# Latent attention with a factored feed-forward layer on one core: the order of work at a unit's boundary, and pair 0's weights later in the start-up

## The chip, the cores and the metric

The kernel runs on one core of one Trainium2 chip. The metric is the device time of one launch in microseconds (us). Engines are called as in the profile: PE is TensorE, PEld its weight loads, DVE is VectorE, ACT is ScalarE, POOL is GpSimd, SP is SyncE, which issues nearly all DMAs here.

## The reference, cut to what matters

```python
xn = layernorm(x)                               # x: 1 x 2048 x 512
q = (xn @ wq)            -> 16 heads, 128 (nope) + 64 (rope)
kva = xn @ wkv_a         -> ckv (128), k_pe (64)
ckv = ckv * rsqrt(mean(ckv^2) + 1e-6) * kv_norm_scale
kv = (ckv @ wkv_b)       -> 16 heads, k_nope 128 + v 128
q_pe, k_pe = rope(q_pe), rope(k_pe)
scores = (q_nope k_nope^T + q_pe k_pe^T) / sqrt(192), causal
out = softmax(scores) @ v                       # 16 heads x 128
attn = out @ wo
mixed = sum over 8 factors of xn @ factors[r], / sqrt(8) + bias
return x + attn + mixed
```

## The kernel before

The weights are absorbed. For a head h, w_abs = wq_nope[h] x wkv_b_k[h] takes the normalized x straight to a query of the 128-wide latent, and w_vo = wkv_b_v[h] x wo[h] takes the latent output straight to the 512-wide result, so all heads share one set of keys (kTh, kTl, the rope part kRh, kRl) and values (vH, vL). Every operand is split into a high and a low half-precision part, and a product is three matmuls (`three`, L358 to L360: high x high, high x low, low x high); the products w_abs, w_vo and the output projection use the fp32r format.

*Start-up.* A loop of steps t = 0 to 19 on every engine. A step normalizes and transposes one tile of 128 rows of x, and two steps later projects it to the latent (L429); every second step finishes a pair of tiles: scaling, rope, keys (L439), values. Between these, in fixed steps, stands the preparation of head pair 0: GpSimd's `scale_keys(0)` (L1179), ScalarE's `squares` of the weights (L646), TensorE's `norm` sum over partitions (L395), VectorE's `row_powers` and `scale_pair` (L841 to L867), the transposes of wq and wkv_b (L377, L384), `w_abs` and `w_pe`. GpSimd meanwhile adds up the eight factors of the feed-forward layer (L1160).

*Units.* A unit i is one head of one chunk of 512 queries: 64 units, chunks in the order 3, 2, 1, 0, sixteen heads each. A unit has four rows r of 128 queries. Chunk 3 sees 2048 keys, four pieces of up to 512 a row; chunk 0 sees up to 512, one piece a row. For each piece TensorE makes scores (L493 to L499) in one of four score banks, VectorE takes the maximum (L1017, the masked last piece L1019), after the last piece the row maximum (L1029) and the exponential's bias nm (L1035), ScalarE the exponential (`exps`, L703) and its half-precision high part (`high_parts`, L713), GpSimd the low part (`low_parts`, L1218), and SP issues the DMA that transposes both into pT. The values product of unit i-1 (tiles pT, vH, vL) runs in the later rows of unit i and ends in its row 3 with one bank of outputs. `read_output` then splits it: ScalarE casts the high part into oT (L720), VectorE subtracts for the low part (L1048). In rows 0 to 3 of unit i+1 TensorE makes the four output projections of that head (`head_output`, tiles wV, oT), and VectorE accumulates each into the result (L1062).

*The order of the work.* Each engine runs its own instruction list in order, and only semaphores tie the lists together. What is not scores, maxima, exponentials or low parts comes from one function, `fills(i, r)`: the list of extra work of row r of unit i, behind the row's main work. Every engine walks the same list and takes the kinds that concern it: "q" (the next unit's query: TensorE projects it, tiles xT, wA; ScalarE casts, L686; VectorE forms the low part, L994), "pe" (rope queries of a pair), "parts" (their parts: ScalarE L692, GpSimd L1209), "out" (an output projection), "pv" (the values product and, at its end, `read_output`), "den" (denominators), and, in the first sixteen units only, the preparation of later heads' weights: "wo" (ScalarE's cast of wo, L682) and "wo_low" (GpSimd's low part of it, L1190), "wvo" (TensorE's w_vo product, tiles wV, wKV; VectorE's split of it, L937), "tq", "tkv", "wabs", squares ("sqk", "sq0", "sq1", "sqp"), "nrm", "wpe". The three PSUM banks for this work rotate in the order of the same list (`bank_order`): each use waits for VectorE to have read the use three before. In unit 0 stands the feed-forward product, whose weights follow from the squares of the summed factors ("sqf", "nf").

ScalarE differs in one point: in rows 0 and 1 of a unit with three or four pieces, it does the row's extra work after its third exponential (p == 2), in front of the fourth (L798 to L800). VectorE does all extra work after the row's maxima and nm (L1141 to L1145), so the low part of an output stands at the end of row 3, in front of the next unit's row 0 (L1070 to L1072).

Of the kernel before, what the change touches and what calls it, by code (L numbers as in the profile page):

```python
# [35 lines left out]
NU = NC * H  # L36
# [50 lines left out]
def fills(i, r):  # L87

    out = []
    if r == 0:  # L90
        if 1 <= i <= H:
            out.append(("wo", i - 1))
# [4 lines left out]
    if r == 0:  # L97
        if i + 1 < NU:
            out.append(("q", i + 1))
        if i + 2 <= H + 2:  # L100
            out.append(("tkv", i + 2))
        if i % 2 == 0 and i + 2 < H:
            out += [("sqk", i + 2), ("r8", i + 2)]
        if i == 0:
            out.append(("sqf", 0))
        if i // H == NC - 1 and i + 1 < NU and (i + 1) % H:
            out.append(("parts", i + 1))
# [5 lines left out]
    if r == 1:  # L113
        if i % 2 == 0 and i + 2 < H:
            out += [("nrm", i + 2), ("wpe", i + 2)]
        if i == 0:
            out.append(("nf", 0))
        if i + 2 < H:
            out.append(("tq", i + 2))
        if 1 <= i <= NU:  # L120
            out.append(("den", i - 1))
        if i // H < NC - 1 and i + 1 < NU and (i + 1) % H:
            out.append(("parts", i + 1))
        if 1 <= i <= H:
            out.append(("wo_low", i - 1))
        if i % 2 and i + 3 < H:
            out.append(("sqp", i + 3))
# [32 lines left out]
def bank_order():  # L160

    pre = []
    for t in range(NT + 4):
        if t < NT:
            pre.append(("xt", t))
        if t == 0:
            pre.append(("na", 0))
        if t == 3:
            pre.append(("nrm", 0))
        if t in (4, 8):  # L170
            pre += [("tq", t // 4 - 1), ("tkv", t // 4 - 1)]
        if t in (6, 10):
            pre.append(("wabs", t // 4 - 1))
        if t % 2 == 1 and 0 <= t // 2 - 2 < NP:
            pre.append(("kT", t // 2 - 2))
        if t == NT + 1:
            pre.append(("pe", 0))
        if t == NT + 2:
            pre.append(("q", 0))
# [4 lines left out]
def build(nc, x, wq, wkv_a, wkv_b, wo, kvs, factors, bias, rope_t, rope_n, out):  # L184
    ctx = ExitStack()
    with ctx:
# [169 lines left out]
        def _(e):  # L356
# [201 lines left out]
            for t in range(NT + 4):  # L558
# [5 lines left out]
                if t == 3:  # L564
                    norm(("nrm", 0), ("a_sqp", "a_sq0", "a_sq1", "v_r8"), nrm[:, :])
                if t in (4, 8):
                    wq_transpose(t // 4 - 1)
                    kv_transpose(t // 4 - 1)
                if t in (6, 10):
                    w_abs(t // 4 - 1)  # L570
# [18 lines left out]
        def _(e):  # L589
# [164 lines left out]
            for t in range(NT + 4):  # L754
# [12 lines left out]
                if t == 2:  # L767
# [4 lines left out]
                if t == 3:  # L772
                    squares("sq1", 0)
                    squares("sqp", 0)
                if t == 8:
                    w_pe(0)
# [14 lines left out]
            for i in range(NU + 2):  # L791
                for r in range(QT):
                    last = chunk(i) if i < NU else -1
                    for p in range(last + 1):
# [3 lines left out]
                        if p == 2 and r < 2:  # L798
                            for kind, n in fills(i, r):
                                fill(kind, n)  # L800
                    if last >= 0:
                        high_parts(i, r, last)
                    if last < 2 or r >= 2:
                        for kind, n in fills(i, r):
# [4 lines left out]
        def _(e):  # L809
# [255 lines left out]
            def fill(kind, n):  # L1065
# [4 lines left out]
                elif kind == "pv":  # L1070
                    if n[1].stop == QT * (chunk(n[0]) + 1):
                        read_output(n[0])  # L1072
# [27 lines left out]
            for t in range(NT + 4):  # L1100
# [11 lines left out]
                if t == 2:  # L1112
# [3 lines left out]
                if t == 3:  # L1116
                    scale_pair(0)
                if t in (4, 8):
                    wq_transpose(t // 4 - 1)
                    kv_transpose(t // 4 - 1)  # L1120
                if t in (6, 10):
                    w_abs(t // 4 - 1)
                if t % 2 == 0 and 0 <= p - 2 < NP:
                    value_parts(p - 2)
                if t == 9:
# [12 lines left out]
            for i in range(NU + 2):  # L1138
                for r in range(QT):
# [4 lines left out]
                    for kind, n in fills(i, r):  # L1144
# [4 lines left out]
        def _(e):  # L1149
# [63 lines left out]
            def low_parts(i, r, p):  # L1213
# [18 lines left out]
                            pattern=[[-1, CH]], channel_multiplier=1).then_inc(z["g_const"], 1)  # L1232
            for i in range(NF):
                factor(i)
                if i == KE + 3:
                    scale_keys(0)
# [278 lines left out]
```

## Time and profile before

| | us |
|---|---|
| median of 3 runs | 1705.14 (1702.17 to 1706.04) |
| profiled execution | 1705.76 |
| its span | 1703.7 |
| TensorE, VectorE, ScalarE, GpSimd busy | 1547.7, 1012.0, 955.6, 913.3 |
| mean granted TensorE clock | 0.979 |

The span is the time from the first to the last instruction of the profiled execution. "Idle before" in a row is the time in which the engine stood still before the instruction, with what ended it; "issue" means that the profile shows no releaser. Times of a row in a timeline are its start and its duration.

### The profile page before, as it was taken

The numbers are of one execution on the slowest core, as the hardware profiler recorded it, in microseconds if no ns is written. First come the engines' busy times: TensorE is split into PE (matmuls) and PEld (weight loads), VectorE is DVE, ScalarE is ACT, GpSimd is POOL, SyncE is SP. The second block draws the span as 40 slices with busy tenths as digits, with TensorE's granted clock in tenths as the row PEclk, the third lists the DMA queues.
The fourth block names the chain that finished last, engine by engine and source line by source line (L and its number), as shares of the span: only waits on it lengthen the run. The fifth ranks groups of instructions, "written<-read, shape, count | busy, mean of one in ns | idle before, by whom it ended". The sixth has DMA issues, their size and how long they took to land.

```text
span 1703.7 us, 25255 instructions
## 1 busy us (share of the span) xinstructions
PE 1547.7 (91%) x7876; PEld 821.2 (48%) x7876; DVE 1012.0 (59%) x2356; ACT 955.6 (56%) x2329; POOL 913.3 (54%) x897
## 2 busy tenths in 40 slices
PE   4779899999999999999999999999999999988887
PEld 3534454544445454444444454444444544444444
DVE  5855566565665665556555565556556665656666
ACT  5654656666666556655665656655455555443443
POOL 3555555655556555565555565556445555443443
PEclk9889999999999999999999999999999999999999
DMA  8626676777677778677786777967656668454554
GB/s 276 210 43 137 127 152 145 155 146 152 146 143 142 144 155 185 136 157 152 159 158 140 143 144 132 192 131 174 128 132 133 135 133 168 112 134 94 112 113 119
DMA packets 646883, 246.68 MB, mean 145 GB/s; under 512 B 599392, under 2 KB 612192, under 8 KB 646112
## 3 DMA queue, kind: packets, MB, share of 16 engines
q1 hardware_dynamic: 646752, 245.08, 67.5%
q8 instruction: 65, 1.06, 0.3%
q14 instruction: 66, 0.54, 0.1%
HBM read 79.30 MB, written 23.07 MB: 60 GB/s over the span
## 4 chain that ended last, share of the span: by engine, by line
PE 74%; DVE 9%; issue 8%; ACT 7%; POOL 1%; DMA 1%; SPq 0%; ACTq 0%; DVEq 0%; POOLq 0%
PE ps L358 16%; PE ps L360 15%; PE ps L359 15%; PE ps L493 6%; PE ps L498 6%; PE ps L499 6%; PE ps L494 6%; PE ps L495 6%; ACT ex L703 4%; DVE gm L1017 2%; DVE ps L1019 2%; DVE acc L1062 1%; ACT q L686 1%; DVE nm L1035 1%; ACT st L713 0%
## 5 line engine op out<-in xcount | busy, mean ns | idle before, releaser
L1218 POOL TENSOR_TENSOR st<-ex,st 128x512 f16<-128x512 f32 (+3 forms) x640 | 636.8, 1013 | 635.9 <-ACT st L713 625.4
L703 ACT ACTIVATE ex<-ps,nm,scales 128x512 f32<-128x512 f32 (+3 forms) x640 | 452.0, 708 | 610.3 <-DVE nm L1035 610.3
L713 ACT ACTIVATE st<-ex 128x512 f16<-128x512 f32 (+3 forms) x640 | 342.1, 561 | 6.1 <-ACT ex L703 0.4
L1017 DVE TENSOR_REDUCE gm<-ps 128x1 f32<-128x512 f32 (+1 forms) x384 | 248.6, 667 | 141.5 <-PE ps L499 139.8
L493 PE MATMUL ps<-kTh,q 128*128 128x512 f16 (+3 forms) x640 | 225.4, 352 | 16.3 <-ACT ex L703 12.4
L498 PE MATMUL ps<-kRh,q 128*128 128x512 f16 (+3 forms) x640 | 223.9, 350 | 3.7 <-POOL q L1209 3.7
L494 PE MATMUL ps<-kTl,q 128*128 128x512 f16 (+3 forms) x640 | 224.4, 351 | 0.0
L495 PE MATMUL ps<-kTh,q 128*128 128x512 f16 (+3 forms) x640 | 224.1, 350 | 0.0
L499 PE MATMUL ps<-kRl,q 128*128 128x512 f16 (+3 forms) x640 | 223.9, 350 | 0.0
L358 PE MATMUL ps<-pT,vH 128*128 128x512 f16 (+3 forms) x640 | 223.2, 349 | 0.0
L359 PE MATMUL ps<-pT,vH 128*128 128x512 f16 (+3 forms) x640 | 222.2, 347 | 0.0
L360 PE MATMUL ps<-pT,vL 128*128 128x512 f16 (+3 forms) x640 | 218.9, 347 | 0.0
L358 PE MATMUL ps<-wV,oT 128*128 128x512 f32 x256 | 131.8, 515 | 72.9 <-issue 67.6
L1062 DVE SCALAR_TENSOR_TENSOR acc<-ps,rden,acc 128x512 f32<-128x512 f32 x256 | 189.5, 742 | 14.0 <-PE ps L360 13.6
L1209 POOL TENSOR_TENSOR q<-rot,q 32x512 f16<-32x512 f32 x128 | 149.2, 1166 | 63.4 <-ACT q L692 51.5
L994 DVE SCALAR_TENSOR_TENSOR q<-ps,q 128x512 f16<-128x512 f32 x64 | 44.2, 691 | 194.9 <-ACT q L686 194.9
L1019 DVE CUSTOM_DVE_ANT_0 ps<-ps,cmask 128x256 f32<-128x256 f32 (+3 forms) x256 | 132.3, 517 | 28.4 <-PE ps L499 25.3
L1048 DVE TENSOR_TENSOR oT<-ps,oT 128x512 fp32r<-128x512 f32 x64 | 44.2, 691 | 137.2 <-ACT oT L720 137.2
L703 ACT ACTIVATION_READ_ACCUMULATOR ex<-ps,nm,scales 128x1 f32 x640 | 125.2, 196 | 0.0
L493 PEld LDWEIGHTS ps<-kTh,q 128*128 128x128 f16 x640 | 62.9, 98 | 95.2 <-ACT ex L703 24.4
L358 PE MATMUL ps<-xT,wA 128*128 128x512 f16 x256 | 104.7, 409 | 0.0
L360 PE MATMUL ps<-wV,oT 128*128 128x512 f32 x256 | 102.7, 401 | 0.0
(187 smaller groups left out, 2307.5 us busy)
## 6 DMA issues: line engine op xcount, KB each, us to landing
wV<-w_vo SPq DMA_DIRECT2D x48, 512.0 KB, 3.6
wA<-w_abs SPq DMA_DIRECT2D x48, 256.0 KB, 2.9
pT<-st SPq DMA_TRANSPOSE x640, 3.2
early<-factors_in SPq DMA_DIRECT2D x32, 256.0 KB, 3.7
w_vo<-wV SPq DMA_DIRECT2D x16, 512.0 KB, 3.1
wP<-w_pe SPq DMA_DIRECT2D x24, 256.0 KB, 3.0
wsq<-wq_in SPq DMA_DIRECT2D x16, 256.0 KB, 3.5
wso<-wo_in SPq DMA_DIRECT2D x16, 256.0 KB, 2.8
```

Of the source, the lines that this page charges most:

```text
L358: e.matmul(o, a[0], b[0], start=first, stop=False)
L359: e.matmul(o, a[0], b[1], start=False, stop=False)
L360: return e.matmul(o, a[1], b[0], start=False, stop=last)
L493: e.matmul(b, q[:, i % 2, 0, qs], kTh[:, ks], start=True, stop=False)
L494: e.matmul(b, q[:, i % 2, 0, qs], kTl[:, ks], start=False, stop=False)
L495: e.matmul(b, q[:, i % 2, 1, qs], kTh[:, ks], start=False, stop=False)
L498: e.matmul(b, q[:, i % 2, 2, qs], kRh[:, ks], start=False, stop=False)
L499: e.matmul(b, q[:, i % 2, 2, qs], kRl[:, ks], start=False, stop=True).then_inc(z["p_s"], 1)
L703: e.activation(ex[:, n % NEX, 0:keys], s_bank(n)[:, 0:keys], ACT.Exp, bias=nm[:, (i * QT + r) % 4:(i * QT + r) % 4 + 1], scale=scales[:, p ...
L713: e.activation(stage(n, keys)[:, :, 0, :], ex[:, n % NEX, 0:keys].rearrange("p (t n) -> p t n", n=P), ACT.Copy).then_inc(z["a_pH"], 1)
L1017: e.tensor_reduce(m, b, AX_X, ALU.max).then_inc(z["v_max"], 1)
L1218: e.tensor_tensor(s[:, :, 1, :], ex[:, n % NEX, 0:keys].rearrange("p (t n) -> p t n", n=P), s[:, :, 0, :], ALU.subtract).then_inc(z["g_pL" ...
```

## The change

- `fills`: in row 0 "q" now stands before "wo" and "out", on every engine that follows the list and in the rotation of the PSUM banks. "wo_low" goes from row 1 to row 0.
- VectorE: the output's low part leaves the end of row 3 and follows the next unit's row 0 maxima and nm. In units 0 to 15 it then takes "out" before the other kinds; in units 16 and later it follows the list, "q" before "out".
- ScalarE: in front of the fourth exponential of rows 0 and 1 it keeps only "q", "wo" and "parts"; other kinds follow the row.
- GpSimd: `scale_keys(0)` stands before the first factor sum instead of among them.
- Start-up: pair 0's squares go from steps 2 and 3 to 3 and 5, the norm and the pair's scales from 3 to 7, the row powers from 2 to 4, the transposes of wq and wkv_b from 4 and 8 to 5 and 9, w_abs from 6 and 10 to 8 and 11, w_pe from 8 (ScalarE) and 9 (VectorE) to 12 and 13.

```diff
@@ fills(i, r)
     if r == 0:
+        if i + 1 < NU:
+            out.append(("q", i + 1))
         if 1 <= i <= H:
-            out.append(("wo", i - 1))
+            out += [("wo", i - 1), ("wo_low", i - 1)]
     if i == NU - 1:
         out += [("out", (i - 2) * QT + t) for t in range(QT) if r == 3]
     elif 2 <= i:
         out.append(("out", (i - 2) * QT + r))
     if r == 0:
-        if i + 1 < NU:
-            out.append(("q", i + 1))
...
-        if 1 <= i <= H:
-            out.append(("wo_low", i - 1))
@@ start-up, TensorE (bank_order, ScalarE and VectorE alike)
-                if t == 3:
-                    norm(("nrm", 0), ("a_sqp", "a_sq0", "a_sq1", "v_r8"), nrm[:, :])
-                if t in (4, 8):
+                if t in (5, 9):
                     wq_transpose(t // 4 - 1)
                     kv_transpose(t // 4 - 1)
-                if t in (6, 10):
-                    w_abs(t // 4 - 1)
+                if t == 7:
+                    norm(("nrm", 0), ("a_sqp", "a_sq0", "a_sq1", "v_r8"), nrm[:, :])
+                if t in (8, 11):
+                    w_abs(t // 3 - 2)
@@ ScalarE, units
                         if p == 2 and r < 2:
+
                             for kind, n in fills(i, r):
-                                fill(kind, n)
+                                if kind in ("q", "wo", "parts"):
+                                    fill(kind, n)
                     if last >= 0:
                         high_parts(i, r, last)
-                    if last < 2 or r >= 2:
-                        for kind, n in fills(i, r):
+                    for kind, n in fills(i, r):
+                        if last < 2 or r >= 2 or kind not in ("q", "wo", "parts"):
                             fill(kind, n)
@@ VectorE, fill and units
-                elif kind == "pv":
-                    if n[1].stop == QT * (chunk(n[0]) + 1):
-                        read_output(n[0])
...
                         row_max(i, r)
-                    for kind, n in fills(i, r):
+                    if r == 0 and 2 <= i:
+                        read_output(i - 2)
+
+                    for kind, n in sorted(fills(i, r), key=lambda work: i < H and work[0] != "out"):
                         fill(kind, n)
@@ GpSimd
+            scale_keys(0)
             for i in range(NF):
                 factor(i)
-                if i == KE + 3:
-                    scale_keys(0)
```

## Rows read from the trace of the kernel before

**Rows 1.** The page's busy times: us (share of the span) xinstructions.
```profile
PE 1547.7 (91%) x7876; PEld 821.2 (48%) x7876; DVE 1012.0 (59%) x2356; ACT 955.6 (56%) x2329; POOL 913.3 (54%) x897
```
**Rows 2.** Waits of TensorE, 160:721, 721:1686, 1686:1704: us in total, times, longest.
```profile
PE ps L358 <- issue: 28.7, 23, 2.1
PE ps L493 <- ACT ex L703: 8.6, 14, 0.8
...
PE ps L358 <- issue: 60.7, 33, 3.3
PE ps L498 <- POOL q L1209: 1.6, 1, 1.6
...
PE ps L358 <- DVE oT L1048: 2.9, 2, 1.5
```
**Rows 3.** TensorE's groups, 160:721, then 721:1686: busy, mean ns | idle before.
```profile
L358 PE MATMUL ps<-wV,wKV 128*128 128x512 f32 x15 | 7.2, 480 | 20.7 <-issue 20.7
...
L358 PE MATMUL ps<-wV,oT 128*128 128x512 f32 x189 | 98.1, 519 | 60.4 <-issue 59.7
```
**Rows 4.** Timeline of a unit boundary, 817 to 823: start us, us.
```profile
817.49 0.27 PE L499 MATMUL ps<-kRl,q 128*128 128x256 f16 x1
...
818.09 0.59 ACT L720 ACTIVATE oT<-ps 128x512 fp32r<-128x512 f32 x1
818.72 0.69 DVE L1048 TENSOR_TENSOR oT<-ps,oT 128x512 fp32r<-128x512 f32 x1 [3.83 <-ACT oT L720]
...
819.51 0.47 PE L358 MATMUL ps<-wV,oT 128*128 128x512 f32 x1 [1.75 <-issue]
...
820.28 0.39 PE L358 MATMUL ps<-xT,wA 128*128 128x512 f16 x1
...
820.39 0.42 DVE L1019 CUSTOM_DVE_ANT_0 ps<-ps,cmask 128x256 f32<-128x256 f32 x1
...
821.09 0.22 DVE L1035 SCALAR_TENSOR_TENSOR nm<-rm,scales,head 128x1 f32<-128x1 f32 x1
...
822.88 0.38 PE L493 MATMUL ps<-kTh,q 128*128 128x512 f16 x1
```
**Rows 5.** Timeline at a w_vo product.
```profile
436.73 1.26 POOL L1190 TENSOR_TENSOR wV<-wso,wV 128x512 fp32r<-128x512 f32 x1
...
438.09 0.47 PE L358 MATMUL ps<-wV,wKV 128*128 128x512 f32 x1 [1.71 <-issue]
```
**Rows 6.** 13 stretches with a low clock: busy by engine, granted clock, DMA; one and their sum.
```profile
1585.20:1588.60 3.40, 1.42 (x4) 0.80 (x5) 1.17 (x4) 1.97 (x5) 1.16 (x1) 0.83 0.78 186
...
sum 44.30, PE 25.86 PEld 15.13 DVE 26.39 ACT 19.94 POOL 26.44; mean PE 1.99 PEld 1.16 DVE 2.03 ACT 1.53 POOL 2.03
```
**Rows 7.** Timeline of a unit boundary of the last chunk.
```profile
1584.53 0.22 PE L499 MATMUL ps<-kRl,q 128*128 128x128 f16 x1
...
1586.39 0.69 DVE L1048 TENSOR_TENSOR oT<-ps,oT 128x512 fp32r<-128x512 f32 x1 [1.48 <-ACT oT L720]
...
1587.18 0.56 PE L358 MATMUL ps<-wV,oT 128*128 128x512 f32 x1 [2.44 <-issue]
```
**Rows 8.** VectorE's group of the query's low part, 721:1700.
```profile
L994 DVE SCALAR_TENSOR_TENSOR q<-ps,q 128x512 f16<-128x512 f32 x46 | 31.8, 691 | 131.0 <-ACT q L686 131.0
```
**Rows 9.** Timeline, row 1's last scores of an even unit.
```profile
422.16 0.28 PE L493 MATMUL ps<-kTh,q 128*128 128x256 f16 x1 [0.76 <-ACT ex L703]
```
**Rows 10.** Waits of TensorE, 0:160.
```profile
PE ps L493 <- ACT ex L703: 3.8, 4, 2.0
```
**Rows 11.** Start-up: timeline, then a window (busy PE, PEld, DVE, ACT, POOL).
```profile
24.70 0.42 ACT L646 ACTIVATE sqr<-wsk 128x256 bf16<-128x256 f32 x1 [8.18 <-POOL wsk L1179]
...
28.33 0.34 PE L395 MATMUL ps<-nrm,ones 128*128 128x4 f32 x1 [8.52 <-ACT sqr L646]
...
36.80:72.00 35.20, 23.67 (x174) 21.03 (x173) 33.34 (x81) 22.81 (x63) 24.15 (x20) 0.81 0.72 225
```
**Rows 12.** VectorE's line of nm: duration ns min/median/max.
```profile
L1035 DVE SCALAR_TENSOR_TENSOR nm<-rm,scales,head x192: 218/220/1152, 100.6 to 1458.7; 128x1 f32<-128x1 f32 x192
```

More of the change, by code:

```diff
@@ L167, in bank_order @@
             pre.append(("na", 0))
-        if t == 3:
+        if t in (5, 9):
+            pre += [("tq", t // 4 - 1), ("tkv", t // 4 - 1)]
+        if t == 7:
             pre.append(("nrm", 0))
-        if t in (4, 8):
-            pre += [("tq", t // 4 - 1), ("tkv", t // 4 - 1)]
-        if t in (6, 10):
-            pre.append(("wabs", t // 4 - 1))
+        if t in (8, 11):
+            pre.append(("wabs", t // 3 - 2))
         if t % 2 == 1 and 0 <= t // 2 - 2 < NP:
@@ L563, in _ @@
                     norm(("na", 0), ("a_sqa",), nra[:, :])
-                if t == 3:
-                    norm(("nrm", 0), ("a_sqp", "a_sq0", "a_sq1", "v_r8"), nrm[:, :])
-                if t in (4, 8):
+                if t in (5, 9):
                     wq_transpose(t // 4 - 1)
                     kv_transpose(t // 4 - 1)
-                if t in (6, 10):
-                    w_abs(t // 4 - 1)
+                if t == 7:
+                    norm(("nrm", 0), ("a_sqp", "a_sq0", "a_sq1", "v_r8"), nrm[:, :])
+                if t in (8, 11):
+                    w_abs(t // 3 - 2)
                 if t % 2 == 1 and 0 <= p - 2 < NP:
@@ L766, in _ @@
                     value_parts(p - 2)
-                if t == 2:
+                if t == 3:
                     e.wait_ge(z["a_sqa"], 1)
@@ L771, in _ @@
                     squares("sq0", 0)
-                if t == 3:
+                if t == 5:
                     squares("sq1", 0)
                     squares("sqp", 0)
-                if t == 8:
+                if t == 12:
                     w_pe(0)
@@ L1111, in _ @@
                                            op0=ALU.mult, op1=ALU.subtract).then_inc(z["v_wa"], 1)
-                if t == 2:
+                if t == 4:
                     e.wait_ge(z["d_scl"], 16)
@@ L1115, in _ @@
                     row_powers(0)
-                if t == 3:
-                    scale_pair(0)
-                if t in (4, 8):
+                if t in (5, 9):
                     wq_transpose(t // 4 - 1)
                     kv_transpose(t // 4 - 1)
-                if t in (6, 10):
-                    w_abs(t // 4 - 1)
+                if t == 7:
+                    scale_pair(0)
+                if t in (8, 11):
+                    w_abs(t // 3 - 2)
                 if t % 2 == 0 and 0 <= p - 2 < NP:
                     value_parts(p - 2)
-                if t == 9:
+                if t == 13:
                     w_pe(0)
```

## The prediction

> **What bounds the kernel now.** I read the page's busy shares first. TensorE works 1547.7 of 1703.7 us, the other three engines 913 to 1012 us [rows 1]. TensorE bounds, and the question is what its 156 us of idle time (1703.7 - 1547.7) wait for.
>
> So its waits come next, asked for by stretch. From 160 to 721 us (the 16 units of the first chunk worked) it waits 28.7 us for "issue" and 8.6 us for ScalarE's exponentials; from 721 to 1686 us 60.7 us for "issue" and once 1.6 us for GpSimd; in the last 18 us 2.9 us for VectorE's oT [rows 2]. "Issue" names no releaser, so I ask which matmul stood behind the wait. By tile there are only two: the first matmul of the w_vo product (wV,wKV) with 20.7 us in the first stretch, and that of an output projection (wV,oT) with 60.4 us in the second [rows 3]. The first stretch's other 8.0 us (28.7 - 20.7) are wV,oT too, in 8 waits of 23, and about 1.0 us of the second is the last w_vo product.
>
> Then one unit boundary in order of time [rows 4]. The last score matmul of the new unit's row 0 ends at 817.76. ScalarE casts the outputs from 818.09 to 818.68, VectorE forms their low part from 818.72 to 819.41, and at 819.51, after 1.75 us of idling, TensorE starts the output projection. Behind it come the twelve matmuls of the next unit's query projection, 820.28 to 822.88 (start of the following scores): 2.60 us of work that needs nothing of this output.
>
> The w_vo wait is as plain [rows 5]: GpSimd's low part of wo ends at 437.99 (436.73 + 1.26), and TensorE starts at 438.09 after 1.71 us of idling.
>
> Last the clock. Each of 13 stretches of 3.4 us, at one of these waits, shows a granted clock of 0.83, the mean of its two levels (1.2 and 2.4 GHz) in the stretch; the 13 hold 25.86 us of TensorE work [rows 6].
>
> **The change, part by part.**
>
> *Query projection ahead of the output projection, output's low part behind the row's maxima.* The 2.60 us now lie between the scores and the output projection. The low part has to be ready at their end. VectorE can begin the masked maximum when the scores end (817.76); from it to the end of nm are 0.92 us (820.39 to 821.09 + 0.22, [rows 4]), and with one more piece still to do (a maximum of 512 columns is taken as 0.69, like the low part of that size) the row is finished at 819.4 at the latest. The cast is done by 818.68, so the low part ends at 820.1, 2.3 us after the scores: covered. In the last 16 units (one piece a row) the scores end at 1584.75, the low part (behind ScalarE's cast) at 1587.08, and the projection waits 2.44 us [rows 7]: just covered. I leave 0.2 us in every second of them, 1.6 us, and 1.0 us for the two or three longest waits (up to 3.3 us, [rows 2]). 8.0 + 59.7 ("issue" of [rows 3]) - 2.6 = 65.1; I take 65. The last two heads have no query projection to put there, so their 2.9 us stay. Bounds: all of 68.4, or 28 if the low part came 1 us beyond the cover at each of the 40 boundaries that wait (8 and 32).
>
> In units 16 and later VectorE also takes the query's low part, for which it waits on ScalarE (131.0 us over 46, [rows 8]), before the output's accumulation, an operation of the same size (0.69). Row 1's maxima stood behind the query's low part already; the accumulation is added in front of them, the output's low part of 0.69 is gone from in front of row 0's. Only a PSUM bank, three uses on, waits for the accumulation. Cost 0; at worst 0.69 x 48 = 33 us, if row 1 were critical.
>
> *Low part of wo one row earlier.* GpSimd's 1.26 us go from behind row 1 to behind row 0; the engine is busy 54% [rows 1]. TensorE comes for the result in row 2, a row or more later. Behind the moved instruction are queued row 1's low parts of the exponentials, and behind those SP's transposes, needed only in the next unit; ScalarE's stage buffers are eight deep. SP's next load of wo starts earlier, in front of the loads of wk and wq. The 20.7 + 1.0 us go; bounds 15 and 21.7, I take 21.
>
> *ScalarE keeps only query, wo and rope parts between the pieces.* In even units of the first chunk a sum of squares stood before row 0's last exponential, and TensorE waited 0.76 us behind that one [rows 9]; a wP cast does the same in row 1. Both now follow, and row 0's exponentials start earlier. I take 7 of the 8.6 us; bounds 3 and 8.6. Before 160 us, mostly in unit 0, the same wait is 3.8 us [rows 10], but there the displaced sum of the factors' squares is itself needed for the feed-forward weights of row 2: 1.5, bounds 0 and 3.8.
>
> *Clock.* Without the waits the low stretches in the body should go. 25.86 us of work at half speed is 12.9 us lost. The 1.6 us for GpSimd's rope part stays [rows 2], and with it one low stretch: 11, bounds 0 and 12.9.
>
> *Start-up.* ScalarE waits 8.18 us, until 24.70, for GpSimd's scaling of pair 0's key weights, which stands behind four factor sums; TensorE's norm sum waits 8.52 us for ScalarE, until 28.33, with the x transposes queued behind it [rows 11]. The diff takes the norm from step 3 to step 7 and the scaling ahead of the factors, so the 8.5 us go. VectorE's chain for pair 0 comes back: ten operations on single columns, of which nm is one by size with 0.22 us [rows 12], so 2 us at most; today they lie where VectorE would wait anyway, while from 36.8 to 72 us VectorE is the bound (33.34 of 35.20 us busy) [rows 11]. Net 7 (8.5 less the chain at 0.15 us an operation). Bounds: 3, if the copies of the two weight transposes (some 2 us: two of 0.69 like the low part in [rows 4], two smaller) and a further wait come back as well; 12, if VectorE, freed, also gets the later x statistics out of the way. w_abs and w_pe shift within that same stretch: 0, as VectorE's sum in it stays. GpSimd's factor sums come 0.6 us later; unit 0 needs the last of them only after the steps.
>
> Sum: 65 + 21 + 7 + 1.5 + 11 + 7 = 112.5 us. The profiled execution took 1705.76 us (span 1703.7), 0.6 above the median of 1705.14. 1705.1 - 112.5 = 1592.6; I say 1592.
>
> *A rule that speaks against it.* The row first: VectorE's nm, 128x1, takes 220 ns in the median but up to 1152 [rows 12]. The Trainium skill (SBUF — State Buffer, "SBUF: two separate sides") has VectorE and GpSimd share a port pair that is locked for a whole instruction, against a VectorE operation with two SBUF inputs. By it GpSimd's moved 1.26 us can meet row 1's nm in 16 units, 16 x 0.93 us (1152 - 220 ns) = 15 us, giving 1607 if nothing hides it; by the rows' slack it costs nothing.
>
> **Rivals.**
>
> 1. *Half the cover* (1630). ScalarE's cast of the outputs stands behind its own exponentials; if TensorE, now faster, outruns that chain, each boundary keeps a wait and the clock dips with it. Half of 65 and of 11 is 38 us: 1630; a third, 25 us, gives 1617. For it: 2.60 against 2.44 leaves 0.16 us in the last 16 units [rows 4, 7]. Against: the other units have 0.5 us and more.
>
> 2. *Slower: VectorE's row 1 becomes the loop* (1729). In units 16 to 63 the accumulation and row 1's maxima wait behind the query's low part. If the four score banks fill meanwhile, TensorE stops at row 2. Today's wait is 131.0 / 46 = 2.85 us [rows 8]; on TensorE's path that is 48 x 2.85 = 137 us. It decides from 112.5 / 48 = 2.3 us a unit. Against: VectorE is busy 59% [rows 1], and the query projection, hence ScalarE's cast, comes earlier.
>
> 3. *It doesn't do what it says* (1703). The low part behind the maxima moves TensorE's wait behind the query projection at its old length, and GpSimd's earlier low part is held up by ScalarE's wo cast, which now follows the query's. For it: little; VectorE stood idle 3.83 us before the low part [rows 4], so it has the time.
>
> 4. *More than forecast* (1577). Every part at its upper bound: 68.4 + 21.7 + 8.6 + 3.8 + 12.9 + 12 = 127.4.
>
> **How the numbers follow.** Forecast, with its own range of 1580 to 1606: 0.72. Half the cover 0.16, more than forecast 0.07, slower 0.03, no effect 0.02. The range takes in the upper bounds and the beginning of the half cover: 1576 to 1618. Some 3.4 us (0.2%) is about what a measurement of this kernel can tell from no change. Faster 0.95, same 0.02, slower 0.03.
>
> **What would show it.** Right: waits before wV,oT between the first unit and the last two under 5 us in all, none before wV,wKV; the query's matmuls directly behind row 0's scores; the clock low once or twice after 160 us; ScalarE's squares behind row 0's last exponential; no 8 us wait for a norm, and unit 0's first score matmul 7 us earlier. Wrong: if TensorE's busy and idle time together stay above 1606 us. Then its waits by tile name the step: wV,oT again (rival 1), scores of row 2 behind exponentials (rival 2), or a new name.

## The result, and the profile after

| us | before | after |
|---|---|---|
| median | 1705.14 | 1571.87 (1569.92 to 1576.8, 4 runs) |
| profiled execution, its span | 1705.76, 1703.7 | 1576.8, 1574.7 |
| mean granted TensorE clock | 0.979 | 0.988 |

The ratio is 0.9226, with a 95% interval of 0.9202 to 0.925: 133 us less, where 112.5 were forecast, and 4 us below the range. The profiled execution of after is its slowest; the spans differ by 129.0 us. Lines of after stand one or two lower than before: L356 to L358 for the helper's three matmuls, L491 to L497 for the scores, L684 and L718 for ScalarE's casts of queries and outputs.

The page of after answers to [rows 1]: TensorE is busy 33.7 us less for the same 7876 matmuls, and idle 60.7 us in place of 156.

```profile
PE 1514.0 (96%) x7876; PEld 819.7 (52%) x7876; DVE 1033.9 (66%) x2356; ACT 952.3 (60%) x2329; POOL 915.3 (58%) x897
```

The waits of TensorE by stretch answer to [rows 2]: 145:656, 656:1556 and 1556:1580, each in us in total, times, longest.

```profile
PE ps L356 <- DVE q L994: 2.4, 1, 2.4
PE ps L393 <- DVE nrm L843: 2.1, 6, 0.7
PE ps L491 <- ACT ex L701: 0.4, 2, 0.3
...
PE ps L356 <- issue: 2.8, 8, 0.4
PE ps L496 <- POOL q L1209: 1.6, 1, 1.6
...
PE ps L356 <- DVE oT L1048: 1.5, 1, 1.5
PE ps L356 <- issue: 1.5, 1, 1.5
PE ps L356 <- DVE acc L1062: 0.9, 1, 0.9
```

By tile (answering to [rows 3]; busy, mean ns | idle before), 145:656, then 656:1556:

```profile
L356 PE MATMUL ps<-wV,oT 128*128 128x512 f32 x55 | 29.8, 542 | 0.0
L356 PE MATMUL ps<-wV,wKV 128*128 128x512 f32 x15 | 8.7, 583 | 0.0
...
L356 PE MATMUL ps<-wV,oT 128*128 128x512 f32 x191 | 102.2, 535 | 3.0 <-issue 2.8
```

All 21.7 us before wV,wKV are gone, and of the 72.9 us before wV,oT in the whole run 6.9 are left, 3.8 of them in the last two heads. The timeline of a unit boundary (answering to [rows 4]) shows why:

```profile
868.96 0.27 PE L497 MATMUL ps<-kRl,q 128*128 128x256 f16 x1
869.07 0.38 PE L356 MATMUL ps<-xT,wA 128*128 128x512 f16 x1
...
869.27 0.43 DVE L1019 CUSTOM_DVE_ANT_0 ps<-ps,cmask 128x256 f32<-128x256 f32 x1
...
869.55 0.59 ACT L718 ACTIVATE oT<-ps 128x512 fp32r<-128x512 f32 x1
...
869.98 0.40 DVE L1035 SCALAR_TENSOR_TENSOR nm<-rm,scales,head 128x1 f32<-128x1 f32 x1
...
870.31 0.68 DVE L1048 TENSOR_TENSOR oT<-ps,oT 128x512 fp32r<-128x512 f32 x1
...
871.47 0.58 PE L356 MATMUL ps<-wV,oT 128*128 128x512 f32 x1
```

The query's twelve matmuls start right behind the scores; under them VectorE finishes nm and then the output's low part, at 870.99, and the output projection follows with no idle time, 0.48 us later. In the last chunk an even unit (answering to [rows 7]) is covered all but 0.36 us: VectorE waits for ScalarE's cast, which stands behind an exponential and its high part, and the low part ends at 1499.18. In the odd units TensorE does not wait.

```profile
1496.12 0.22 PE L497 MATMUL ps<-kRl,q 128*128 128x128 f16 x1
1496.17 0.38 PE L356 MATMUL ps<-xT,wA 128*128 128x512 f16 x1
...
1498.49 0.69 DVE L1048 TENSOR_TENSOR oT<-ps,oT 128x512 fp32r<-128x512 f32 x1 [0.96 <-ACT oT L718]
...
1499.29 0.47 PE L356 MATMUL ps<-wV,oT 128*128 128x512 f32 x1 [0.36 <-issue]
```

Windows of after, cut where the first score matmul of units 1, 16, 32 and 48 starts (busy PE, PEld, DVE, ACT, POOL; then granted clock, DMA share, GB/s): between units 16 and 47 TensorE has no more to give up than 0.4 us.

```profile
145.00:664.00 519.00, 514.01 (x2647) 276.51 (x2646) 343.76 (x749) 338.10 (x827) 321.38 (x309) 1.00 0.78 160
664.00:1065.90 401.90, 401.90 (x2036) 207.78 (x2034) 231.04 (x540) 256.43 (x627) 243.33 (x235) 1.00 0.78 159
1065.90:1367.70 301.80, 301.41 (x1567) 161.23 (x1565) 207.61 (x476) 175.52 (x435) 173.26 (x173) 1.00 0.74 155
```

The same cuts in all kernels, as lengths in us (from each profiled execution):

| | start-up | unit 0 | 1 to 15 | 16 to 31 | 32 to 47 | 48 on | median, us | ratio, 95% |
|---|---|---|---|---|---|---|---|---|
| before | 91.6 | 55.8 | 559.2 | 421.2 | 332.2 | 243.8 | 1705.14 | |
| after | 85.8 | 59.3 | 519.0 | 401.9 | 301.9 | 206.9 | 1571.87 | .9226 (.9202 to .925) |
| a_boundary | 92.3 | 54.8 | 539.1 | 403.1 | 301.9 | 207.0 | 1600.41 | .9393 (.9376 to .9411) |
| b_wolow | 91.8 | 55.8 | 531.9 | 419.9 | 333.4 | 244.0 | 1676.07 | .9836 (.9815 to .9857) |
| c_act | 92.5 | 57.5 | 557.5 | 421.2 | 330.5 | 240.4 | 1701.05 | .9983 (.9972 to .9994) |
| d_start | 82.3 | 57.3 | 557.6 | 421.6 | 333.6 | 243.4 | 1697.08 | .9961 (.9948 to .9974) |
| e_qonly | 91.5 | 55.1 | 572.9 | 415.1 | 302.0 | 217.6 | 1655.63 | .9706 (.9675 to .9736) |
| f_readonly | 90.7 | 56.2 | 556.5 | 441.2 | 342.9 | 263.7 | 1755.56 | 1.0289 (1.0263 to 1.0316) |
| g_unit0 | 80.6 | 58.2 | 518.9 | 401.9 | 301.8 | 207.1 | 1570.36 | .9208 (.9184 to .9231) |
| h_late | 84.6 | 57.1 | 596.0 | 492.5 | 368.6 | 252.5 | 1853.43 | 1.0867 (1.084 to 1.0895) |
| i_nosort | 82.2 | 56.9 | 517.1 | 401.9 | 301.9 | 207.0 | 1571.24 | .9221 (.9205 to .9238) |
| k_improved | 82.8 | 59.9 | 514.5 | 401.9 | 301.9 | 207.0 | 1570.44 | .9210 (.9194 to .9226) |
| m_row1 | 84.5 | 59.9 | 514.5 | 401.9 | 302.7 | 207.0 | 1569.89 | .9198 (.9184 to .9212) |
| n_both | 80.3 | 57.9 | 514.6 | 401.9 | 301.9 | 207.1 | 1567.21 | .9186 (.9172 to .92) |

### The profile page after: what moved, and what is told of

It is laid out like the page before. It is cut to its first block, busy times and chain, and to the rows that moved or that the text cites. A ratio compares the mean times of both kernels' runs of the same rounds, so it can differ in the third digit from the quotient of the medians.

```text
span 1574.7 us, 25255 instructions
## 1 busy us (share of the span) xinstructions
PE 1514.0 (96%) x7876; PEld 819.7 (52%) x7876; DVE 1033.9 (66%) x2356; ACT 952.3 (60%) x2329; POOL 915.3 (58%) x897
## 4 chain that ended last, share of the span: by engine, by line
PE 86%; DVE 6%; ACT 4%; issue 2%; POOL 1%; DMA 0%; SPq 0%; ACTq 0%; DVEq 0%; POOLq 0%
PE ps L356 17%; PE ps L358 17%; PE ps L357 17%; PE ps L491 7%; PE ps L496 7%; PE ps L497 7%; PE ps L492 7%; PE ps L493 7%; ACT ex L701 2%; DVE gm L1017 1%; DVE ps L1019 1%; DVE kt L966 1%; DVE acc L1062 0%; DVE nm L1035 0%; DVE stats L813 0%
## 5 line engine op out<-in xcount | busy, mean ns | idle before, releaser
L1017 DVE TENSOR_REDUCE gm<-ps 128x1 f32<-128x512 f32 (+1 forms) x384 | 252.0, 669 | 209.7 <-PE ps L497 205.8
L491 PE MATMUL ps<-kTh,q 128*128 128x512 f16 (+3 forms) x640 | 225.1, 352 | 5.5 <-DVE kRl L981 3.6
L497 PE MATMUL ps<-kRl,q 128*128 128x512 f16 (+3 forms) x640 | 223.4, 349 | 0.0
L356 PE MATMUL ps<-pT,vH 128*128 128x512 f16 (+3 forms) x640 | 223.2, 349 | 0.0
L358 PE MATMUL ps<-pT,vL 128*128 128x512 f16 (+3 forms) x640 | 218.9, 347 | 0.0
L356 PE MATMUL ps<-wV,oT 128*128 128x512 f32 x256 | 136.2, 532 | 6.9 <-issue 4.3
L491 PEld LDWEIGHTS ps<-kTh,q 128*128 128x128 f16 x640 | 62.7, 98 | 84.6 <-issue 27.8
L356 PEld LDWEIGHTS ps<-pT,vH 128*128 128x128 f16 x640 | 62.3, 97 | 79.3 <-issue 27.3
L358 PE MATMUL ps<-wV,oT 128*128 128x512 f32 x256 | 101.4, 396 | 0.0
L357 PE MATMUL ps<-wV,oT 128*128 128x512 f32 x256 | 101.0, 395 | 0.0
```

Of the source, the lines that this page charges most:

```text
L356: e.matmul(o, a[0], b[0], start=first, stop=False)
L357: e.matmul(o, a[0], b[1], start=False, stop=False)
L358: return e.matmul(o, a[1], b[0], start=False, stop=last)
L491: e.matmul(b, q[:, i % 2, 0, qs], kTh[:, ks], start=True, stop=False)
L497: e.matmul(b, q[:, i % 2, 2, qs], kRl[:, ks], start=False, stop=True).then_inc(z["p_s"], 1)
L1017: e.tensor_reduce(m, b, AX_X, ALU.max).then_inc(z["v_max"], 1)
```

## The experiments

The first four each make one part of the change in the kernel before. "Ledger" in the expectations is a second working, made when the trace of after was known: it adds to the idle time some 0.22 us a wait, and 1.7 us for each stretch at half clock. So it isn't a forecast of the whole, but each part is a test of it.

**a_boundary.** Queries first, and the output's low part behind the row's maxima, with VectorE's order.

```diff
 fills: +if i + 1 < NU: out.append(("q", i + 1))   (first in row 0)
 VectorE: -elif kind == "pv": ... read_output(n[0])
+if r == 0 and 2 <= i: read_output(i - 2)
+for kind, n in sorted(fills(i, r), key=lambda work: i < H and work[0] != "out"):
```

> The kernel before with the boundary part alone: query projection first in row 0, output's low part behind row 0's maxima, VectorE's sorted extra work. Everything else as before. Ledger theory: the 66 us of waits before wV,oT go, each of the 40-odd removed waits gives 0.22 us more than its idle time (the drain of the matmul before it) = 9, and 11 of the 13 low-clock stretches (3.41 us, each fully busy at half speed, 1.7 us lost) go = 18.7; one new wait of 2.4 us at the entry of the 16th unit: 91 less, 1614. Theory of the prediction: 65 less for the waits and 9 for the clock, 1631.

Measured 1600.41 us, -105.2 against 1705.60 for the kernel before, run beside it. Its stages from unit 32 on are those of after. This part alone takes away 66 us before wV,oT, but also 4.2 us before wV,wKV and most of the waits for exponentials (8.8 to 1.1 us from 145 us on). The latter go with the output's low part from in front of row 0's maxima: f_readonly below, with that move alone, has 1.1 us of them too. The time at half clock from unit 1 to 63 falls from 44.4 to 10.2 us. The working of the prediction (1631 with the half of the clock term that belongs here) missed 30 us, the ledger of the two traces 14.

**b_wolow.** The low part of wo in row 0.

```diff
-out.append(("wo", i - 1))        (row 0)
+out += [("wo", i - 1), ("wo_low", i - 1)]
-out.append(("wo_low", i - 1))    (row 1)
```

> The kernel before with GpSimd's low part of wo in row 0 alone. Ledger theory: 21.7 us of waits, 15 x 0.22 of drain = 3.3, two low-clock stretches (3.4): 28 less, 1677. Theory of the prediction: 21 to 23 less, 1683. If part of it only moves to another wait (the product's operands from VectorE): 1690.

Measured 1676.07, -29.5: the 21.7 us before wV,wKV go and nothing takes their place. They were 15 waits, and the part gives 7.8 us more than their idle time. Its expectation of 1677, made from the ledger, holds; the prediction's 21 is too small by 8.5.

**c_act.** ScalarE's order alone.

```diff
 if p == 2 and r < 2:
     for kind, n in fills(i, r):
-        fill(kind, n)
+        if kind in ("q", "wo", "parts"): fill(kind, n)
 (the other kinds follow the row's last high part)
```

> The kernel before with ScalarE's order alone (only query, wo, parts in front of the fourth exponential). Ledger theory: 8.4 us of waits behind the fourth exponential and 14 x 0.22 go, but unit 0 gets 3.5 us longer, because the sum of the factors' squares is late for the feed-forward weights: 8 less, 1697. Theory of the prediction: 8.5 less with unit 0 1.5 us shorter. The time hardly tells them apart, unit 0's length does: 59 against 54 us (55.75 before).

Measured 1701.05, -4.6. TensorE's waits in 145:1690, of c_act:

```profile
PE ps L358 <- issue: 85.8, 56, 3.3
PE ps L395 <- DVE nrm L844: 4.3, 6, 0.7
PE ps L493 <- ACT ex L703: 3.2, 9, 0.5
```

The waits for exponentials fall from 8.8 to 3.2 us, but the norm sums, whose squares now come after the row, wait 4.3 us in place of 0.7 (in short waits): 3.6 of the 5.6 us come back as a new wait. In after they wait 2.1 us. The waits before wV,wKV fall from 21.7 to 18.2 us here. The expectation set unit 0's length as the test, 59 us by the ledger against 54 by the prediction: it is 57.5, longer than before's 55.8, so the prediction's gain of 1.5 us there is refuted.

**d_start.** The start-up's order alone.

```diff
-if t in (4, 8): wq_transpose, kv_transpose     +if t in (5, 9)
-if t == 3: norm / scale_pair(0)                +if t == 7
-if t in (6, 10): w_abs                         +if t in (8, 11)
 GpSimd: +scale_keys(0)  (ahead of the factors)
```

> The kernel before with the start-up part alone. Ledger theory: the first score matmul comes 5.8 us earlier and nothing else changes: 1699. Theory of the prediction: 7 us, 1698. Rival: unit 0 gives part of it back, since the sum of the factors and its squares are not earlier: 1702.

Measured 1697.08, -8.5. The norm's matmul comes at 31.52 with no idle time before it (8.52 us before it in [rows 11]), and unit 0 starts at 82.3 in place of 91.6 us. The time fits 1698 and 1699 alike; unit 0 gives 1.5 us back.

```profile
20.63 0.41 ACT L646 ACTIVATE sqr<-wsk 128x256 bf16<-128x256 f32 x1
...
31.52 0.28 PE L395 MATMUL ps<-nrm,ones 128*128 128x4 f32 x2
```

The four parts by themselves sum to 147.8 us against 133.3 together. Most of the 14.5 us counted twice can be named: a_boundary and c_act take 7.7 and 5.6 us from the 8.8 us of waits for exponentials, where after takes 8.4 in all, and they take 4.2 and 3.6 us from the waits before wV,wKV, which b_wolow takes away whole.

**e_qonly and f_readonly.** The boundary part, split: only the place of "q" in the list, and only the place of the output's low part.

```diff
 e_qonly:    +("q", i + 1) first in row 0, VectorE as before
 f_readonly: read_output(i - 2) behind row 0's maxima, list as before
```

> The kernel before with the query projection first in row 0 alone; VectorE's low part of the output stays at the end of row 3 and its extra work in list order. If the query projection is the cover and the place on VectorE only a refinement: the low part is ready earlier than in the change, all 66 us of waits and the clock go, and as the row's maxima still stand behind it by 0.7 to 1.4 us that nobody waits for: within 5 us of the boundary part alone, about 1616. If the move on VectorE is needed, because the late maxima hold up ScalarE and the score banks: 1630 or more, with waits behind the exponentials in row 1.

> The kernel before with only VectorE's low part of the output moved behind row 0's maxima; the output projection stays first. The low part ends 0 to 0.7 us later than before and TensorE has nothing to do meanwhile: the waits before wV,oT stay or grow (up to 63 x 0.7 = 44 us): 1700 to 1745. If the earlier maxima were what paid: 1690 or less.

Measured 1655.63 (-50.7) and 1755.56 (+49.3). Together, with VectorE's sort, they gave -105.2: the move of the low part costs 49 us without the cover, and with it (and the sort) brings 54.5 more. Why e_qonly keeps waits is seen on VectorE and ScalarE at a boundary (timeline of e_qonly):

```profile
339.61 0.60 ACT L720 ACTIVATE oT<-ps 128x512 fp32r<-128x512 f32 x1
...
340.24 0.69 DVE L1048 TENSOR_TENSOR oT<-ps,oT 128x512 fp32r<-128x512 f32 x1 [5.12 <-ACT oT L720]
340.85 1.74 DVE L1017 TENSOR_REDUCE gm<-ps 128x1 f32<-128x512 f32 x3
...
343.22 0.22 DVE L1035 SCALAR_TENSOR_TENSOR nm<-rm,scales,head 128x1 f32<-128x1 f32 x1
343.47 0.78 ACT L703 ACTIVATE ex<-ps,nm,scales 128x512 f32<-128x512 f32 x1 [2.65 <-DVE nm L1035]
...
344.39 0.39 PE L493 MATMUL ps<-kTh,q 128*128 128x512 f16 x1 [0.52 <-ACT ex L703]
```

VectorE stands idle in front of the output's low part while the three full pieces of row 0 lie ready, then does their maxima in 1.74 us; nm is late, ScalarE waits 2.65 us for it, and TensorE waits for the exponentials: 21.4 us over 38 waits before the first matmul of a score piece from unit 1 to 63, against 8.9 over 16 before. I had expected about 1616 by the cover alone; it was the other case that I had written down, that the move is needed.

In f_readonly TensorE's waits before wV,oT grow from 72.9 us over 51 to 125.3 over 64: behind the maxima, with nothing of TensorE's to cover it, the low part is simply later.

**g_unit0.** After, with ScalarE's old order in unit 0 alone.

```diff
-if kind in ("q", "wo", "parts"):
+if i == 0 or kind in ("q", "wo", "parts"):
```

> The changed kernel with ScalarE's old order in unit 0 alone (sum of the factors' squares and their high part in front of the fourth exponential again). Ledger theory: unit 0's 59.3 us go back to about 55.8, 3.5 less: 1568. Rival, that unit 0 is long because the sum of the factors comes late relative to the shortened start-up: no change, 1572.

Measured 1570.36 against 1571.87 of after: 1.5 us less, but the intervals of the ratios overlap nearly whole. Unit 0 took 58.2 us, not the 55.8 expected, against 59.3. Inconclusive by itself; see n_both and point 6 below.

**h_late.** After, with the output's low part on VectorE behind the query's low part, and its fills in list order (i_nosort shows that this order alone is worth nothing). A test of the cover: it asks what happens when it runs out.

```diff
-if r == 0 and 2 <= i: read_output(i - 2)
+if r == 0 and i == NU - 1: read_output(i - 2)
-for kind, n in sorted(fills(i, r), key=...):
+for kind, n in fills(i, r):
+    if r == 0 and kind == "out": read_output(i - 2)
     fill(kind, n)
```

> The changed kernel with the output's low part on VectorE behind the query's low part, which waits for ScalarE's cast of the query. The order on TensorE is that of the change. TensorE then waits before wV,oT in all 62 boundaries, some 2 to 3 us each. Ledger theory: 62 x (2.5 + 0.2) = 167 us and low-clock stretches of 1.7 us in a third to a half of the boundaries, 35 to 50 us: 1575 + 210 = about 1780, slower than before. If waits of this length do not lower the clock: 1740, with a granted clock of 0.99. If the cover still reaches: 1572.

Measured 1853.43. A boundary of h_late:

```profile
902.14 0.59 ACT L684 ACTIVATE q<-ps 128x512 f16<-128x512 f32 x1
...
902.76 0.69 DVE L994 SCALAR_TENSOR_TENSOR q<-ps,q 128x512 f16<-128x512 f32 x1 [3.55 <-ACT q L684]
903.37 0.68 DVE L1048 TENSOR_TENSOR oT<-ps,oT 128x512 fp32r<-128x512 f32 x1
904.15 0.76 PE L356 MATMUL ps<-wV,oT 128*128 128x512 f32 x1 [3.37 <-issue]
```

The low part now waits for ScalarE's cast of the query, which comes behind exponentials of the row, and TensorE waits for the low part in nearly every unit: 183.3 us over 64 waits. From unit 1 to 63 that is 172 us of idle time more than in after, and the time grew by 281.6. The rest is mostly clock: 225.3 us of this stretch are at half clock, in place of 3.4. I expected 1780 and mis-sized the clock again, at 35 to 50 us for what is some 100 (0.44 x 221.9 by the fit below is 98).

**i_nosort.** After, with VectorE's fills in list order in every unit.

```diff
-for kind, n in sorted(fills(i, r), key=lambda work: i < H and work[0] != "out"):
+for kind, n in fills(i, r):
```

> The changed kernel with VectorE's fills in list order in every unit (no sort): in units 2 to 15 the output's sum of a row (about 0.8 us) stands behind the query's low part and the transposes' copies again. What it asks: of the 133 us, is anything due to the sort? Theory A (the gain is the cover that query projection gives to the low part of the latent output, and the sort only frees a bank of PSUM somewhat earlier): TensorE's idle time in the body rises by less than 3 us, span 1574 to 1580, ratio to the kernel before 0.922 to 0.926. Rival B (the sort is a part of the gain: with it gone the output's bank is handed on late, as in the run with queries first alone, where units 1 to 15 took 573 us in place of 519): waits before the latent output or the query's projection of 0.5 us and more return in units 2 to 15, their stage grows from 519 to 530 us or more, span 1586 or more.

Measured 1571.24 against 1571.87, the same waits, the same stages but for the clock: the sort is worth nothing here. So it was the move that e_qonly lacked, as far as the sort's worth in after tells. Its wait before wP of 2.4 us is still there, yet in this execution no stretch at half clock follows it, and units 1 to 15 take 517.1 in place of 519.0 us.

**k_improved, m_row1, n_both.** Two edits that the trace of after suggests, together (k), the first alone (m), and the first with g_unit0's order (n). The first takes away the new wait before wP, where the rotary projection of unit 16 is put in the PSUM bank of query 16, just cast (timeline of after):

```profile
633.92 0.59 ACT L684 ACTIVATE q<-ps 128x512 f16<-128x512 f32 x1
634.55 0.69 DVE L994 SCALAR_TENSOR_TENSOR q<-ps,q 128x512 f16<-128x512 f32 x1 [0.89 <-ACT q L684]
...
635.29 0.39 PE L356 MATMUL ps<-xT,wP 128*128 128x512 f16 x1 [2.42 <-DVE q L994]
```

```diff
-return (e - 1, 0) if e % H == 0 else (e - 2, 3)                  (pe_at)
+return (e - 1, int(e == H)) if e % H == 0 else (e - 2, 3)        (k, m, n)
-if i == 0: ("sqf", 0) in row 0, ("nf", 0) in row 1; ("sqk", 2) in row 0
+if i == 0: ("nf", 0) in row 0                                    (k)
+squares("sqk", 2); factor_squares()  (ScalarE, ahead of unit 0)  (k)
```

> The changed kernel and two more edits that its trace suggests. (1) The rotary projection of unit 16's queries goes from row 0 to row 1 of unit 15, where it no longer takes the bank of PSUM that query 16 has just been put in: the wait of 2.42 us before wP at 635.29 goes, and with it the 3.4 us at half clock right behind it (3.41 us of work there, so 1.7 us), and some 0.2 us of the matmul that ran out ahead of it: -4.3 us. (2) The sum of squares of the feed-forward factors goes from unit 0 to the end of the start-up on ScalarE, and their norm and scale from row 1 to row 0 of unit 0: the wait of 2.65 us before the first feed-forward matmul at 114.74 goes with the 2.8 us at half clock behind it (1.4 us), -4 us, or less if ScalarE's sum of 2048 squares (some 2 us) now delays the first exponentials of unit 0. Theory A: both go, 1563 to 1566 us. Rival B: the first edit gives its 4.3 us and the second only moves the wait to row 0: 1567 to 1569. Rival C: the rotary projection in row 1 is late for its two rows of ScalarE and GpSimd work ahead of unit 16, and the wait comes back before unit 16's first scores: 1570 or more.

> The changed kernel with one edit alone: the rotary projection of unit 16's queries stands in row 1 of unit 15 (row 0 before). In the run that had this edit and another, units 1 to 15 took 514.5 us in place of 519.0. Theory A: 4.5 us less than the changed kernel, 1567.4 us, ratio 0.919 to 0.920; idle before wP none, no TensorE time at half clock from unit 1 to unit 63. Rival B: the half clock behind that wait comes only in some executions (a run with the same wait of 2.4 us there had none at half clock, and 517.1 us): then the edit gives 2.6 to 4.3 us, and the median is at 1568 to 1569.

> The changed kernel with that edit and ScalarE's old order in unit 0 (there, all fills of a row behind the third exponential, which takes the wait of 2.65 us before the first feed-forward matmul away). Theory A: 4.5 us less than the changed kernel by the first edit and 1.5 by the second (the median of that one alone was 1570.36 against 1571.87): 1566 us. Rival B: the second was within the spread of the start-up (the same code began unit 0's scores at 80.6, 82.2 and 85.8 us in three profiles): then this run and the other of this call have the same time within 1 us.

The first edit did what it says in all three: no wait before wP, units 1 to 15 in 514.5 us (4.5 less than after). The second of k moved the wait: VectorE takes the factors' low part in front of row 1's maxima, first idle for ScalarE's high part, and TensorE waits 7.63 us for exponentials (two timelines of k_improved):

```profile
101.58 2.35 DVE L893 SCALAR_TENSOR_TENSOR early<-early,fsc 128x2048 f16<-128x2048 f32 x1 [1.97 <-ACT early L739]
103.85 1.88 DVE L1017 TENSOR_REDUCE gm<-ps 128x1 f32<-128x512 f32 x3
...
106.61 0.78 ACT L699 ACTIVATE ex<-ps,nm,scales 128x512 f32<-128x512 f32 x1 [5.06 <-DVE nm L1035]
...
107.54 0.61 PE L489 MATMUL ps<-kTh,q 128*128 128x512 f16 x1 [7.63 <-ACT ex L699]
```

So k_improved gives 1570.44, above the 1563 to 1569 of its first two cases (the third, 1570 or more, was for a wait before unit 16's scores, which its trace does not have). m_row1 has 1569.89, only 2.0 us below after and above both its cases (1567.4, and 1568 to 1569): the 4.5 us stand in the stage, but not in the medians. n_both has 1567.21, 2.7 us below m_row1 beside which it ran, which is more than the 1 us that "the second edit is worth nothing" allows and in the direction of g_unit0; the intervals of the two ratios overlap (.9184 to .9212 and .9172 to .92), so this is likely and not shown. n_both is the best kernel of this work by its median: 4.7 us below after, with an interval that ends where that of after begins (.9202).

## Why the prediction was too small

The direction, the place and the idle time were right. Two steps of the sum failed: the price of the clock, put at 11 us, and the price of a wait beyond its idle time, which the sum put at nothing. The second is about as large as the whole clock term was. They can be taken apart with all 14 traces. In each I took the stretch from the first score matmul of unit 1 to that of unit 63, the idle time of TensorE in it, the number of its waits (over 0.02 us), and the time at half clock. A least-squares fit gives

    length = 1390.9 + idle + 0.24 x waits + 0.44 x time at half clock   (us)

and meets twelve of the fourteen within 0.8 us, over a spread of 285 us (the other two, e_qonly and f_readonly, to -2.7 and +2.6):

| | length | idle | waits | at half clock | left over |
|---|---|---|---|---|---|
| before | 1533.0 | 101.4 | 86 | 44.4 | +0.2 |
| after | 1406.9 | 9.4 | 19 | 3.4 | +0.4 |
| a_boundary | 1428.3 | 25.6 | 29 | 10.2 | +0.2 |
| b_wolow | 1505.8 | 79.7 | 71 | 41.0 | -0.2 |
| h_late | 1687.6 | 181.8 | 64 | 225.3 | -0.7 |
| n_both | 1402.6 | 7.2 | 19 | 0.0 | 0.0 |

From before to after these are 92.0 us of idle time, 67 x 0.24 = 16.1 for the waits, 41.0 x 0.44 = 18.0 for the clock: 126.1, as much as the stretch became shorter.

The fit alone does not settle the split. With a free factor on the idle time it gives 1.14, 0.11 a wait and 0.36 for the clock, and meets all fourteen within 0.4 us. But the two terms can also be added up directly, each start of a matmul to the next against the median of that kind of matmul at full clock without a wait. What the waits cost beyond their idle time falls from 16.7 to 3.1 us, and what half clock costs from 21.7 to 1.7; against the median of the same pair of matmuls it is 19.6 to 4.8 and 21.0 to 1.7. So the waits are worth 14 to 15 us and the clock 19 to 20, near the fit's 16 and 18.

1. *The boundary: 65.* Right. The waits before wV,oT gave 66.0 (72.9 to 6.9). The last chunk keeps 0.36 us in every second unit, seven times, where 0.2 was said; the other leftovers, put at 1.0 us, are 0.5.

2. *w_vo: 21.* Right: 21.7.

3. *ScalarE's order: 7.* Right in sum, 8.4 (8.8 to 0.4), but not by ScalarE's order alone: c_act takes 5.6 of it and a_boundary 7.7, each without the other. The squares behind the row cost a wait of 2.1 us that was not in the sum.

4. *Clock: 11.* The first step that failed, with what it measured: 18 by the fit, 19 to 20 added up. The 13 windows stood about 2 us too early. A window with a granted clock of 0.83 is at half clock for only a third of it ((1 - 0.83) / 0.5 = 0.34), so my own row said that most of the low stretch lay outside; I took half of the TensorE work in it all the same. In these 13 half clock begins between 0.4 us before the end of the wait and 2.0 us after it, and TensorE is at work in nearly all of it. The same 13 stretches of before, placed where the clock is low: the first, the one that stood in [rows 6], and the sum.

```profile
174.30:177.70 3.40, 3.40 (x11) 1.48 (x11) 2.67 (x4) 0.00 (x0) 2.21 (x3) 0.50 0.84 135
...
1587.50:1590.90 3.40, 3.40 (x9) 1.26 (x8) 0.84 (x2) 0.86 (x3) 0.43 (x1) 0.51 1.04 155
...
sum 44.20, PE 43.77 PEld 16.84 DVE 15.84 ACT 14.35 POOL 14.60; mean PE 3.37 PEld 1.30 DVE 1.22 ACT 1.10 POOL 1.12
```

PE is busy 43.77 of 44.20 us, not 25.86 of 44.30, at the lower of its two levels (1.2 GHz): half of it is 21.9 us, of which after keeps 1.7 in its single stretch. The fit's 18 lies a tenth below the 20.2 that this makes.

```profile
636.30:639.70 3.40, 3.40 (x10) 1.22 (x8) 0.01 (x1) 0.00 (x0) 2.53 (x3) 0.51 1.17 145
```

5. *Missing: 14 to 16.* The second step that failed: the sum took a wait's price to be its idle time. A wait costs more than its "idle before". Take an even unit of the second chunk, whose first score matmul and the next unit's are these, in before (unit 20) and then in after (unit 22):

```profile
815.15 0.38 PE L493 MATMUL ps<-kTh,q 128*128 128x512 f16 x1
...
843.33 0.38 PE L493 MATMUL ps<-kTh,q 128*128 128x512 f16 x1
```

```profile
816.81 0.38 PE L491 MATMUL ps<-kTh,q 128*128 128x512 f16 x1
...
843.02 0.38 PE L491 MATMUL ps<-kTh,q 128*128 128x512 f16 x1
```

28.18 us became 26.21 (all of these units lie within 0.02 of the one or the other): 1.97 us for a wait listed as 1.75 [rows 4], at full clock in both. The odd units, which had no wait, took 23.6 in both. The reason stands in [rows 4]: the last score matmul of 256 columns starts at 817.49 and is shown for 0.27 us, but in a full pipeline the next starts 0.11 us after it (868.96 to 869.07 above). From start to start the wait cost 2.02 - 0.11 = 1.91 us; the 0.16 between is the matmul's own run-out, which the profile counts as busy. It is not only so in this place: the waits behind score matmuls of 128 and of 512 columns in before cost 0.16 us beyond their idle time too. That is also where the 33.7 us of busy time went that TensorE lost with no matmul removed: 14 to 16 here, 18 to 20 in the clock.

6. *Unit 0: 1.5.* It took 3.5 us longer in this profile, and 1.1 to 4.1 longer in the eight others with the changed start-up, ScalarE's order or both; in the kernels with neither it is 54.8 to 56.2. The first feed-forward matmul waits 2.65 us, where it waited 0.42 before (timeline of after):

```profile
105.92 0.17 DVE L891 RECIPROCAL fsc<-fsc 128x1 f32<-128x1 f32 x1
...
110.11 2.10 ACT L741 ACTIVATE early<-early,eps,fsc 128x2048 f16<-128x2048 f32 x1
...
112.24 2.35 DVE L893 SCALAR_TENSOR_TENSOR early<-early,fsc 128x2048 f16<-128x2048 f32 x1 [6.16 <-ACT early L741]
...
114.74 0.59 PE L356 MATMUL ps<-early 128*128 128x512 f16 x1 [2.65 <-DVE early L893]
```

The squares of the factors, now behind row 0's last exponential, are not what holds it up: the scale that follows from them is ready at 106.09. It is the next step, ScalarE's high part of the factors, which the new order puts behind row 1's last exponential, four microseconds later; VectorE waits 6.16 us for it. The working named the displaced sum of squares (needed for row 2), booked a gain all the same, and did not name the high part. d_start, with the old order, lengthened unit 0 by 1.5 too, so part of it belongs to the earlier start. Start-up and unit 0 together, by the table, are 138.2 to 139.6 us in the three kernels with the new start-up and the old order in unit 0 (d_start, g_unit0, n_both), and 139.1 to 145.1 in the four with both new (after, h_late, i_nosort, m_row1). That points to a cost of the new order in unit 0, of a size that one profile each does not show.

7. *Start-up: 7.* Right within its own spread: the cut between start-up and unit 0 is at 90.7 to 92.5 us in the profiles of the old order and at 80.3 to 85.8 in those of the new, which differ by more than any of my edits between them.

With 18 for the clock, 16 for the waits and the rest as forecast, the sum would have been 135.5 us: 1570 against 1571.87. That is nearer than it deserves. In the two profiles 126.1 of the 129.0 us lie from unit 1 to 63, and start-up and unit 0 together gave 2.3 (147.4 to 145.1), where 8.5 were forecast; the medians differ by 4.3 us more than the profiles, and no stage of a profile shows where.

*The rivals.* Half the cover (1630): refuted in size. Its mechanism, ScalarE's cast behind its own exponentials, is there in every second unit of the last chunk, at 0.36 us each. Slower by VectorE's row 1 (1729): not in after, but h_late shows that the mechanism exists, with the output's low part in that place. More than forecast (1577): this is the case that came, though not by the mechanism given there; the parts stayed near their central values, and the excess is the two terms above. It had 7 in 100. *The rule of the shared port.* In after nm takes up to 1209 ns, against 1152 in [rows 12], and its median over the last chunk is 536 ns, but TensorE waits for exponentials only 0.4 us from unit 1 to 63. So the 15 us that made 1607 did not come. The Trainium skill (SBUF — State Buffer, "SBUF: two separate sides") would have nm locked out by GpSimd's instruction. Whether that is what lengthens nm no run here shows; its price did not reach TensorE.

## What to carry to other kernels

Work that needs nothing of the late operand belongs between the last producer and its consumer, and the operand's chain must then be ordered so that the cover is not spent ahead of it: the two halves of that edit, apart, gave -51 and +49 us, and together -105. When waits of a bound engine go, price each at its idle time plus the run-out of the instruction before it, from start to start of whole periods. And put the clock's price where the clock is low, not where the wait is: a window's granted clock says how much of it is.

## What the runs showed of the hardware

In before, waits of 1.2 to 3.3 us had a stretch of 3.4 us at a granted clock of 0.51 behind them, which began between 0.4 us before the end of the wait and 2.0 us after it, with TensorE busy in 43.77 of 44.20 us; but only 13 of 86 waits had one, and the same 2.4 us before wP had such a stretch behind it in after and none in i_nosort. In h_late, with 64 waits of 2.8 us on average, 225.3 us were at half clock, in 54 stretches of 3.4 or 6.8 us. So the clock's price is not a fixed sum a wait: it was some 0.2 us per wait of before (0.44 x 44.4 / 86), and 1.5 in h_late (0.44 x 225.3 / 64), where the waits are longer. Which property of a wait decides was not tried.
